# One decoder layer on one core: the stages ahead of attention rewritten, with the first head's inputs made there

## What is computed

```python
scale = 1 / max(mean(abs(table)), 1e-5)                 # table: 32000 x 256, read in full
h = clip(round(table * scale), -1, 1) / scale; h = h[ids]          # 2048 x 256
x = layernorm(h)
nq  = rms(x @ w_cq);  q  = [nq @ w_dq_nope, rope(nq @ w_dq_rope)]  # 16 heads x (32 + 64)
ckv = rms(x @ w_ckv); k1 = [ckv @ w_dk_nope, rope(x @ w_krope / 16)]; v1 = ckv @ w_dv
gate = softmax(mean(x @ w_gate))
idx = sort(top_k(x @ w_imp, 64)); ks, vs = projections of x[idx]   # 64 kept tokens
kw, vw = rope(x @ w_wink), x @ w_winv
out = gate0 * attn(q, k1, v1, causal) + gate1 * attn(q, ks, vs) + gate2 * attn(q, kw, vw, causal)
h = h + out @ w_proj
h = h + mixture_of_experts(layernorm(h))                # 8 experts, top 2
```

## Time and profile before

| | us |
|---|---|
| runs, median (3) | 2870.55 (2869.1 to 2880.93) |
| profiled execution | 2868.0 |
| its span on the core | 2866.3 |
| PE busy | 2343.5 (82%) |
| DVE / ACT / POOL busy | 1776.3 / 1757.3 / 1629.4 |

### The profile page before, as it was taken

How to read it: one execution, slowest core, us unless ns; L and a number is a source line. 1 busy time by engine, 2 the same in 40 slices (tenths; PEclk the granted TensorE clock), 3 DMA queues, 4 the chain that set the end, 5 groups by cost and what they waited for, 6 DMA issues and landing times. The chain is left out here.

```text
span 2866.3 us, 37854 instructions
## 1 busy us (share of the span) xinstructions
PE 2343.5 (82%) x12128; PEld 1866.3 (65%) x12128; DVE 1776.3 (62%) x2826; ACT 1757.3 (61%) x3576; POOL 1629.4 (57%) x1408
## 2 busy tenths in 40 slices
PE   0056544999999999999999999999999999357885
PEld 0044323777777777777777777777777777357885
DVE  3528324667677676867767676675766665365553
ACT  3334220776677767777776777777777788105663
POOL 2334342666757666675766667666566566106885
PEclk9975555999999999999999999999999999658998
DMA  9657386433515153250524415043121310605776
GB/s 401 239 166 224 129 275 183 119 79 95 132 29 156 43 136 86 74 137 24 156 63 116 105 55 140 22 112 66 34 65 27 71 33 5 172 32 193 204 199 169
DMA packets 231618, 341.60 MB, mean 119 GB/s; under 512 B 100315, under 2 KB 159179, under 8 KB 218363
## 3 DMA queue, kind: packets, MB, share of 16 engines
q1 hardware_dynamic: 221355, 322.85, 38.3%
q0 software_dynamic: 10064, 16.34, 2.8%
HBM read 228.59 MB, written 110.14 MB: 118 GB/s over the span
## 5 line engine op out<-in xcount | busy, mean ns | idle before, releaser
L1164 POOL TENSOR_TENSOR p_lo<-prob,p_hi 128x512 fp32r<-128x512 f32 (+2 forms) x960 | 1103.5, 1158 | 705.9 <-ACT p_hi L1230 564.7
L1228 ACT ACTIVATE prob<-ps_s 128x512 f32<-128x512 f32 (+4 forms) x1344 | 723.4, 538 | 541.0 <-PE ps_s L1245 420.2
L1363 DVE TENSOR_REDUCE max_part<-ps_x 128x1 f32<-128x512 f32 (+3 forms) x1280 | 742.6, 606 | 212.7 <-PE ps_x L1274 129.6
L1230 ACT ACTIVATE p_hi<-ps_s 128x512 fp32r<-128x512 f32 (+3 forms) x1344 | 716.8, 533 | 1.6
L1164 DVE TENSOR_TENSOR p_lo<-prob,p_hi 128x512 fp32r<-128x512 f32 (+1 forms) x320 | 276.2, 863 | 139.5 <-ACT p_hi L1230 70.8
L1274 PE MATMUL ps_x<-k_hi,q_hi 96*128 96x512 f32 (+3 forms) x640 | 244.4, 382 | 65.3 <-DVE max_part L1363 42.5
L1244 PE MATMUL ps_s<-q_lo,kw_hi 96*128 96x512 f32 (+3 forms) x640 | 256.8, 401 | 0.0
L1244 PE MATMUL ps_s<-q_lo,k_hi 96*128 96x512 f32 (+3 forms) x640 | 252.5, 395 | 0.0
L1328 PE MATMUL ps_o<-p_hi,v_win 128*128 128x512 f32 (+3 forms) x640 | 252.5, 394 | 0.0
L1241 PE MATMUL ps_s<-q_hi,kw_hi 97*128 97x512 f32 (+3 forms) x640 | 247.4, 387 | 3.7 <-DMA q_hi<-neg_max_t 3.7
L1328 PE MATMUL ps_o<-p_hi,v_lat 128*128 128x512 f32 (+3 forms) x640 | 246.2, 385 | 0.0
(11 more groups left out here) (378 smaller groups left out, 4808.5 us busy)
## 6 DMA issues: line engine op xcount, KB each, us to landing
raw<-in_experts_w_dram SPq DMA_DIRECT2D x23, 1536.0 KB
wbuf<-in_tok_weight_dram SPq DMA_DIRECT2D x16, 2000.0 KB, 17.9
v_scratch<-v_split SPq DMA_DIRECT2D x16, 1024.0 KB, 4.5
q_scratch<-st_hi SPq DMA_DIRECT2D x48, 256.0 KB, 4.6
q_scratch<-st_lo SPq DMA_DIRECT2D x48, 256.0 KB, 5.7
kw_scratch<-st_hi SPq DMA_DIRECT2D x48, 256.0 KB, 2.9
kw_scratch<-st_lo SPq DMA_DIRECT2D x48, 256.0 KB, 4.1
q_hi<-q_scratch SPq DMA_DIRECT2D x48, 256.0 KB, 4.8
```

The source lines that it names most:

```text
L1164: ns.tensor_tensor(upper if low else p_lo[:, i % LSLOTS, c:CH], prob[low:P, i % NPROB, c:CH], upper.bitcast(F32), ALU.subtract).then_inc(s ...
L1228: nc.scalar.activation(prob[low:P, i % NPROB, c:CH], ps_s[i % 3][low:P, c:CH], ACT.Exp, scale=SCALE).then_inc(s["p_full"], 1)
L1230: nc.scalar.activation(p_hi[:, i % SLOTS, c:CH], ps_s[i % 3][:, c:CH], ACT.Exp, scale=SCALE).then_inc(s["p_up"], 1)
L1363: ins = nc.vector.tensor_reduce(mpart[:, q, c:c + 1], bank[:, 0:w], axis=AX.X, op=ALU.max)
```

## The change

Five things change. In `embed`, the weights are loaded behind chunk 6 of the scan and split by GpSimd group by group beside it; group 0 stays in SBUF. The small, value and latent weights are also loaded and split there, the rope tables and gains are loaded, thresholds and centring go by quarters, `h0` is stored raw as -1, 0, 1, and the variance comes from the count of non-zeros and the row sum. In `project`, one list `TASKS` of 100 entries sets the order on all engines: four window tasks; 36 tasks of window q/k rest, turned latents, turned rope key and window values; 60 tasks of ranks, q, latent values and latent keys. It makes group 0's q and kw. Six banks go round in a ring, outputs through three buffers. Values are stored unsplit. Comparisons write a 0/1 tile, and TensorE counts them with products of one column. The two rows are turned on TensorE ahead of the store. In `select`, head 0's q and kw are loaded, and its window and selected maxima are taken between the other steps. In `attend`, `FIRST` is gone, head 0 reads the tiles of the selection, and every head's values are rounded by ScalarE and subtracted by GpSimd (`split_up`, `split_low`).

```diff
@@ embed @@
+                if n == WEIGHTS_AT:
+                    sp.dma_start(wq[:].rearrange("p g n -> p (g n)"), a["wq_all"]).then_inc(s["wq"], 16)
...
+            sp.dma_start(g.cos[:], a["cos4"]).then_inc(s["pre"], 16)
...
             for n in range(NG):
+                sp.wait_ge(s["ws"], 4 * (n + 1))
+                sp.dma_start(g.wq_dram[n], wq_s[slot(n)][:].rearrange("p s n -> p (s n)").bitcast(F32)).then_inc(wst[slot(n)], 16)
...
+            for n in range(NG):
+                k = slot(n)
+                if n == 3:
+                    pool.wait_ge(wst[k], 32)
+                kw = wkw[:, :, n, :]
+                nc.gpsimd.tensor_copy(wq_s[k][:, 0, :], wq[:, n, :]).then_inc(s["ws"], 1)
...
+            def threshold(j):
+                c = slice(4 * j, 4 * j + 4)
+                v.add(nc.vector.tensor_scalar(below[:, c, :], rows[:, c, :], scale[:, 1:2], -0.5, ALU.mult, ALU.is_lt))
+                v.wait()
+                v.add(nc.vector.tensor_scalar(rows[:, c, :], rows[:, c, :], scale[:, 1:2], 0.5, ALU.mult, ALU.is_gt))
+                v.wait()
+                for t in range(4 * j, 4 * j + 4):
+                    nc.vector.scalar_tensor_tensor(rows[:, t, :], rows[:, t, :], 1.0, below[:, t, :], ALU.mult, ALU.subtract,
+                                                   accum_out=g.ksum[:, t:t + 1]).then_inc(s["tern"], 1)
@@ project @@
+    kw = [("kw", j, part) for j in range(NJ) for part in (1, 2)]
+    kr = [("kr", j, n) for j in range(NJ) for n in range(2)]
+    values = lambda b: [("v", b, t) for t in range(NT)]
+    first = [("kw", j, 0) for j in range(NJ)]
+    second = merge(kw[:4] + [("lt", j, 0) for j in range(NJ)] + kr + kw[4:], values(WINDOW))
+    third = merge([("rank", c, 0) for c in range(NT)], [("q", j, part) for j in range(NJ) for part in range(3)],
+                  values(LATENT) + [("kn", m, j) for m in range(NG) for j in range(NJ)])
...
+            def count_ranks(c):
+                pe.wait_ge(s["less"], c + 1)
+                for t in range(NT):
+                    last = nc.tensor.matmul(bank[7][:, t:t + 1], less[:, c % 2, t * P:(t + 1) * P], g.ones16[:],
+                                            start=(c == 0 and t == 0), stop=False)
...
+                    nc.scalar.activation(values[:, half, :, j % 8, :], b[:].rearrange("p (h d) -> p h d", h=H), ACT.Copy,
+                                         scale=g.rstd[:, j:j + 1] if i == WINDOW else 1.0).then_inc(s["x_act"], 1)
...
+                v.add(nc.vector.tensor_scalar(less[:, k, 0:n + P], row[:, 0:n + P], sc, None, ALU.is_lt))
+                if n + P < T:
+                    v.add(nc.vector.tensor_scalar(less[:, k, n + P:T], row[:, n + P:T], sc, None, ALU.is_le))
...
-                v.add(nc.vector.tensor_scalar(junk[:, n:T], srow[:, n:T], sc, None, ALU.is_gt, ALU.add, accum_out=g.ranks[:, 0, t:t + 1]))
@@ select @@
+            for n, (half, dram, sem) in enumerate(((q_hi, g.q_dram[0], "q"), (kw_hi, g.kw_dram[0], "kw"), (q_lo, g.q_dram[1], "low"), (kw_lo, g.kw_dram[1], "low"))):
+                for r in range(3):
+                    row = (0, NOPE, NOPE + HALF)[r]
+                    sp.dma_start(half[row:row + NOPE, :].bitcast(F32), dram[0, r, 0:NOPE, :]).then_inc(s[sem], 16)
...
             for n in range(4):
                 for kc in range(KC):
                     w = wk[:, kc, n * CH:(n + 1) * CH] if n < 3 else wv[:, kc, :]
+                    last = nc.tensor.matmul(bank[(3, 4, 5, 2)[n]][0:KEEP, :], selT[:, kc, :], w, start=(kc == 0), stop=(kc == KC - 1))
                 last.then_inc(s["ks"], 1)
+                done = max_products(done, early + (n + 1) * (middle - early) // 4)
...
+            done = max_products(done, len(maxima))
@@ attend @@
+                sp.dma_start(vals[b][:, :, 2 * DV:3 * DV].bitcast(F32), g.v_dram[0 if b == LATENT else 1, h].rearrange("p (t n) -> p t n", n=DV)
...
+            def split_up(h, b):
+                act.wait_ge(s["v_w" if b == WINDOW else "v_l"], 16 * (h + 1))
+                nc.scalar.copy(vals[b][:, :, DV:2 * DV], vals[b][:, :, 2 * DV:3 * DV].bitcast(F32)).then_inc(s["v_up"], 1)
...
+                    if i == SPLIT_L:
+                        split_up(h, LATENT)
+                    if i == SPLIT_W and h + 1 < H:
+                        split_up(h + 1, WINDOW)
...
-            for t in FIRST:
-                pe_task(pe, t)
             pe.wait_ge(s["set"], 5)
```

More of the change, by code:

```diff
@@ new lines, with products @@
+TASKS = front_tasks()
+TIMES = [t for t in TASKS if t[0] != "rank"]
+TN = {t: n for n, t in enumerate(TIMES)}
+RING = 6
+READ_BY = {t: "x_act" if t[0] in ("v", "kn") or t[:1] + t[2:] == ("q", 0) else "x_dve" for t in TIMES}
+READ_NO = {t: sum(READ_BY[u] == READ_BY[t] for u in TIMES[:n + 1]) for n, t in enumerate(TIMES)}
+def products(t):
+    kind, _, part = t
+    if kind == "kn" or (kind in ("q", "kw") and part == 0):
+        return [(t, 0)]
+    if kind in ("q", "kw") and part == 2:
+        return [(t, 1), (t, 2)]
+    return [(t, 0)] if kind == "kr" and part == 1 else []
@@ new lines, with maker @@
+MADE = [o for t in TASKS for o in products(t)]
+MN = {o: n for n, o in enumerate(MADE)}
+NO = 3
+def maker(o):
+    (kind, _, part), r = o
+    return "full_act" if kind == "kn" or (kind == "q" and r == 0) else "full_dve" if kind == "kw" and r == 0 else "full_pool"
+MAKE_NO = {o: sum(maker(u) == maker(o) for u in MADE[:n + 1]) for n, o in enumerate(MADE)}
+TURNS = [t for t in TASKS if t[0] == "kr" and t[2] == 1 or t[0] in ("q", "kw") and t[2] == 2]
+TURN_NO = {t: n for n, t in enumerate(TURNS)}
@@ new lines, in _ @@
+            for n, t in enumerate(TASKS):
+                if n >= 2:
+                    for o in products(TASKS[n - 2]):
+                        store(o)
+                if t == ("rank", 0, 0):
+                    sp.wait_ge(s["llo"], NJ)
+                    for j in range(NJ):
+                        for i, half in enumerate((lat_hi, lat_lo)):
+                            sp.dma_start(g.lat_dram[j, :, i * CH:(i + 1) * CH], half[0:QL, j * CH:(j + 1) * CH].bitcast(F32)).then_inc(s["lst"], 16)
+                before = TASKS[n - 1]
+                if n and before[0] == "v" and before[2] % 8 == 7:
+                    store_values(before[1], before[2] // 8)
@@ new lines, in _ @@
+            made = 0
+            behind = [0, 0]
+            for t in TASKS:
+                lowered = lower(behind.pop(0))
+                if t in TURN_NO:
+                    pool.wait_ge(s["turn"], TURN_NO[t] + 1)
+                    if t[0] == "kr":
+                        sums = [(0, 1, ALU.add)]
+                    else:
+                        sums = [(0, 2, ALU.subtract), (1, 3, ALU.add)]
+                    for o, (x, y, op) in zip(products(t), sums):
+                        n, r = MN[o], rows_of(o)
+                        full_free(pool, n)
+                        nc.gpsimd.tensor_tensor(full[0:r, n % NO, :], turned[0:r, x, :], turned[0:r, y, :], op).then_inc(s["full_pool"], 1)
+                made += len(products(t))
+                behind.append(made)
@@ L364, in _ @@
+            lowered = lower(len(MADE))
+            pool.wait_ge(s["low"], len(MADE))
         @block.tensor
@@ L804, in schedule @@
             spread(h, [("neg", h + 1, 1)], NU - 7, NU - 6)
[L805 to L809 removed]
+    return at
+AT = schedule()
+ALL_X = [t for h in range(H) for i in range(NU) for t in AT.get((h, i), ())]
 XN = {t: n for n, t in enumerate(ALL_X)}
```

932 lines of the change are left out of this document (521 added, 411 removed).

## The result

The changed kernel takes 2779.46 us (median of 4 runs, 2777.27 to 2784.42) against 2871.54 (median of 4, 2869.10 to 2880.93): a ratio of 0.9678, 95% interval 0.9661 to 0.9695. That is 92 us less where 128 were forecast, and inside the range. The profiled execution took 2779.87 us, its span is 2778.1; the sum had 2739.9 for it, so 40 us are to be found.

A forecast was written before the change was run, and what follows sets the result against it. Waits bound the four stages ahead of the loop (no engine over 58% busy), TensorE the loop. Terms -12.6 - 12 + 19.7 - 129.2 + 6 = -128.1 took 2868.0 to 2739.9 us, stated as 2742; range 2692 to 2788.

The forecast's parts named there:

- Table stage: First stage, ahead of the projections: 121 us (116 to 127) instead of 133.6, a change of -12.6.
- Projections: Stage behind the table stage: 39.3 + 46 + 76 + 5 = 166.3 us (140 to 200) instead of 178.5, -12.
- with 5 to drain: End of the projections, behind the third part: 5 us until the stage is over.
- Rival B: Projections: TensorE gets the high clock, GpSimd and DMA bound them at 142 us; total 2718, down to 2692; 22%.
- Rival C: Projections: VectorE and GpSimd alternate, stores wait in a ring of three; stage 200 us, total 2775; 22%.
- A: The forecast itself, whole kernel: 2742 us with 2715 to 2768, projections 166.3; 47%.
- Selection and first pass: Between projections and first score: selection 72 us (62 to 85), +19.7; first pass replaced by 7 (5 to 12), -129.2.
- Head 0: Start of the head loop: 1 us more, since its preparation waits for loads that the kernel before had early.
- 14 heads: Head loop: 5 us more for ScalarE's added value copies and GpSimd's added subtractions, between nothing and 19.
- What would have shown it: Signs across the kernel, among them first score near 360 us instead of 500.6 and head period 121.0 to 122.
- clock 0.5 in the third part: Sign in the projections' third part: granted clock 0.5 speaks for A, near 1 for the high-clock rival.
- E: Head loop: late value loads block ScalarE's exponentials and so TensorE, 32 times, making the kernel slower; 3%.

The follow-up runs named there:

- e5: Changed kernel with four slots instead of three in the two tiles from which the projections' outputs are stored: 2772.70 us.
- e7: Changed kernel with GpSimd leaving out the lower halves of the third part's 28 outputs, except 8 of 512 columns: 2773.59 us.
- e1: Changed kernel with the third part's latent value and kn products over 128 rows instead of 32, the added weight rows zero: 2779.75 us.
- e11: Changed kernel with the edits of e2, e4 and e5, and the ring of unrounded outputs at four as well: 2748.00 us.
- e10: Changed kernel with all edits of e11 and also that of e1: 2750.22 us.
- e4: Changed kernel with ranks counted on VectorE by accumulating compares again, without the rank products on TensorE: 2769.82 us.
- e6: Changed kernel with none of head 0's window maxima between the selection's key products (14 before), all behind the rope: 2785.61 us.
- e2: Changed kernel with head 0's preparation of group 1 starting at unit 11 instead of 6, its latent maxima at 14 instead of 9: 2773.05 us.
- e8: Changed kernel with 8 unused products of 512 columns on TensorE ahead of head 0's first preparation task: 2783.14 us.
- e9: Changed kernel with ScalarE's value copies and GpSimd's value subtractions on one column of 32 from head 1 on: 2778.37 us.
- e12: The kernel before, unchanged, run and traced once more: 2869.98 us.

## Why the prediction was right, and where it was not

**Table stage: right.** 121.7 for 121. Per quarter it is shorter than my 4.8 us, and two collisions with GpSimd's late split of group 3 took their place, as in this row of VectorE, where 0.75 us is the time of the same instruction alone:

```profile
108.46 3.23 DVE L254 TENSOR_SCALAR scratch<-scratch,scale 128x1024 f32<-128x1024 f32 x1
```

One microsecond was too little for that, and the short quarters paid.

**Projections, 183.2 for 166.3: the third part and the drain.** The way to the second part is 40.8 us for 39.3 and the second part 42.1 for 46; the latents' square root starts 32 us in. The third part is 81.9 for 76, but by another sum. The rank products are 0.034 us each, half of what I took; in TensorE's timeline 17 of them lie between these starts:

```profile
241.13 0.39 PE L502 MATMUL b_ps<-ones,less 128*128 128x1 bf16 x7
...
241.71 0.79 PE L538 MATMUL b_ps<-wd_hi,lat_hi 32*128 32x512 f32 x1
```

So TensorE's work is 68 us, not 76; ahead of it I had no term for 13.7 us of waiting for compares. I had sized the compares at 1.7 us a set without a neighbour (at 257.6 us such a set takes 0.94 + 0.55 + 0.35) and put them beside TensorE as covered; they were 3.3 us a set in the mean, and the cover fails where two engines wait for each other by turns. The step that failed most is "with 5 to drain": 18.4, of which the ring of three explains 5.4 (e5) and GpSimd's halves 2.6 (e7), if the two add up; the other 10 are twice my 5.

**Rival B (the high clock in the sequence): no, where it counts.** In the third part and the drain the clock was 0.50 to the end. In the second part it was 0.83, and that part took 42.1 us for 46. The row of 32-row products at 0.50 was the better witness, and e1 shows why: over 128 rows the same stream is granted 0.69. The pair e11 and e10 shows it again: 0.50 with TensorE busy 58.11 of 67.34 us, 0.76 over 128 rows with 42.00 of 66.56. The Trainium skill, TensorE: Matmul & The Clock Gate, "What's actually happening", says that activity releases the throttle, and nothing of rows; the traces agree with it only for products over more rows than 32. The 2692 that B names as its far end isn't its sum: with table stage and selection at their ends (116 and 62) 2718 becomes 2703.

**Rival C (exclusion and ring): right in mechanism, about half in price.** VectorE lost 12 us to GpSimd (e7), the path 4.4 plus 2.6; the ring cost 6. The stage came out between A's 166 and C's 200. That it was cheaper than C fits VectorE's own slack, the 21.5 us in which it waited for TensorE; that is argued, not shown. The Trainium skill, SBUF — State Buffer, "Who interferes with whom", exempts the scalar form that also writes out its accumulator. The trace of e4 agrees, with 2.21 us for 1920 elements beside a busy GpSimd against 2.23 for the plain form in a collision, and 0.94 for 1408 outside one. I quoted the rule against the change and didn't ask what it says of the form being left: beside GpSimd the plain compares lose nearly all that they are faster by (52.6 us against 55.5).

**Selection and first pass: right as a sum, in part by luck.** 82.2 for 79, but two errors stand against each other. Attention's stage starts at 385.0 us, so the selection took 80.1 us for 72 (within its 62 to 85), and the first score comes 2.1 us later, for the 7 (5 to 12) that I gave to the landing and splitting of the values:

```profile
385.01 0.61 SPq L1222 DMA_DIRECT2D v_win<-v_scratch  x1
```

ScalarE's rounding of these values starts at 389.46, behind the first score of 387.07, so the four units of lag cover them; I had put them on the path. In the selection, 14 maxima between the key products cover nothing (e6), so 3 us of the 8 are missing there; the other 5 stay open.

**Head 0, 16.7 for 1: the step that failed.** "Whose preparation waits for loads that before had early" was seen, and priced at 1 us. The stop alone is 3.5 us long; moving the work behind the loads gives 10.3 back (e2), 5.7 of stops and 4.6 of lower clock; filling half of the stop gives nothing (e8). That a late transfer at the head of three engines' lists costs the refilling of the pipeline, with TensorE at the low clock while that lasts, fits both; it is argued, not shown. Of the remaining 6.4 us of head 0 (80.3 against 73.9), 5.0 are busy time of the same 356 products (77.30 us against 72.34, clock 0.89 against 0.94) and 1.4 are stops.

**14 heads, +6.6 for +5: a hit without a reason.** Without the splits that the 5 stood for, the heads took 1722.0 us (e9), no less than the shortest trace with them; the kernel before itself varies by 4.3 (e12), and the changed ones by 6.4. So the term was never measured. What is left, 1.5 us and more (1722.0 and above in every changed trace, 1720.5 at most before), stays open.

**What would have shown it:** first score at 387, not 360; attention's stage was to start at 359 and starts at 385. My 360 was a slip besides: with the 7 us of the first pass the sum gives 366. The mean period of the 14 heads is 123.1 us (122.6 before), outside my 121.0 to 122, which came from one head alone. Of the signs, "clock 0.5 in the third part" was A's and came. E (blocked value copies) did not: ScalarE's value copies never stand among the waits of the loop.

## What to carry to other kernels

Moving work to an idle engine is priced by its instructions and by each crossing of the two engines' lists: here 272 cheap products (9 us of TensorE) cost 11 us, 3.6 for the products and 7.6 for meeting VectorE sixteen times with compares that collide with GpSimd. Check too what the form that you leave was protected from. When a warm-up stage is removed, list the loads that it hid and give their first user a later place; here moving it was worth three times the visible stop. Size a drain by the ring as well as by the bytes: here a fourth slot took 5.4 us off 18.4.

## What the hardware showed unasked

- Products over 32 rows, alone (9.80 of 10 us busy in the kernel before) or mixed with 96-row ones (67.85 of 81.90), stood at a granted 0.50; with zero rows added up to 128, the same columns ran at 0.69 (e1) and 0.76 (e10).
- A bf16 product of one column takes 0.034 us back to back at the low clock (17 in 0.58 us).
- The plain scalar compare of 1408 f32 elements takes 0.94 us alone, the accumulating one 1.68; beside GpSimd's subtractions the sixteen sets took 52.6 and 55.5 us.
- The same program's 14 heads took 1716.2 and 1720.5 us in two executions.
